# First attention phase of a transformer block: projections and score maxima of a sequence placed within one round, and per-head copies of q and k from SBUF to SBUF

## The reference

```python
x = x + _L0_attn_a_ref(_layernorm(x, axis=-1), L0_attn_a_w_qkv, L0_attn_a_b_qkv, L0_attn_a_w_out, L0_attn_a_b_out)
...
qkv = x @ w_qkv + b_qkv
...
scores = jnp.einsum('bhqd,bhkd->bhqk', q, k) * HEAD_DIM ** (-0.5)
scores = jnp.where(mask[None, None], -jnp.inf, scores)
w = jax.nn.softmax(scores, axis=-1)
return jnp.einsum('bhqk,bhkd->bhqd', w, v)
...
return ctx @ w_out + b_out
```

## Time and profile before

| | before |
|---|---|
| median of 3 runs (lowest to highest) | 3182.99 us (3164.28 to 3186.27) |
| the profiled execution | 3179.51 us, of which the span of the profile is 3177.8 us |
| mean granted clock of PE over the span | 0.923 |
| first attention phase | from 0 to about 1078 us |

### The profile page before, as it was taken

One profiled execution on the slowest core, in us unless ns is written; L12 is line 12 of the kernel. 1 busy time (PEld: TensorE's weight loads), 2 busy tenths in 40 slices (PEclk: granted clock), 3 DMA queues, 4 the chain that ended last, 5 costly groups with the idle time before them and its releaser, 6 DMA issues. The chain is left out here.

```text
span 3177.8 us, 57495 instructions
## 1 busy us (share of the span) xinstructions
PE 2720.7 (86%) x17344; PEld 2117.0 (67%) x17344; DVE 1954.4 (62%) x4975; ACT 1375.7 (43%) x2778; POOL 1426.8 (45%) x1603
## 2 busy tenths in 40 slices
PE   5787787877878678988997999999999949999993
PEld 3554454544555457877996777878787739888872
DVE  6565454654556386766565576777777654566664
ACT  1333233332333224645775434333333317666651
POOL 2332232322233253545732543557575535655556
PEclk9998898988989788989998999999999979999996
DMA  6865666665576445657985222334333248888884
GB/s 202 199 167 145 144 155 154 164 149 141 149 171 161 127 146 206 234 178 245 340 293 176 87 77 65 99 112 126 113 123 110 95 156 295 284 300 307 297 279 150
DMA packets 275022, 565.63 MB, mean 178 GB/s; under 512 B 37152, under 2 KB 144800, under 8 KB 273696
## 3 DMA queue, kind: packets, MB, share of 16 engines
q1 hardware_dynamic: 225568, 427.55, 45.0%
q0 software_dynamic: 49152, 134.28, 12.9%
HBM read 275.96 MB, written 285.21 MB: 177 GB/s over the span
## 5 line engine op out<-in xcount | busy, mean ns | idle before, releaser
L513 ACT ACTIVATE a_pt<-a_S 128x384 f32<-128x384 f32 (+3 forms) x640 | 255.2, 452 | 539.2 <-PE a_S L766 539.0
L428 POOL TENSOR_SCALAR_AFFINE_SELECT a_pt<-a_pt 128x512 f32<-128x512 f32 (+1 forms) x320 | 174.6, 546 | 615.3 <-ACT a_pt L513 615.3
L641 DVE TENSOR_REDUCE a_mx<-a_FB 128x2 f32<-128x384 f32 (+4 forms) x512 | 277.6, 592 | 194.3 <-PE a_FB L744 145.6
L1046 POOL DMA_INDIRECT slots<-f_xn,k_picks x256 | 261.6, 1022 | 249.2 <-PE f_Z L1554 98.1
L1829 POOL DMA_INDIRECT k_yg<-made,k_picks x224 | 223.7, 999 | 255.7 <-PE b_Y L2342 139.1
L2624 POOL DMA_INDIRECT f_yg<-made,k_picks x256 | 257.6, 1006 | 169.9 <-PE f_Z L2817 98.4
L779 PE MATMUL a_PV<-a_pt,a_vv 128*32 128x192 f32 (+4 forms) x2048 | 212.8, 394 | 87.1 <-POOL a_pt L435 87.0
L741 PE MATMUL a_FB<-a_kb,a_qb 128*128 128x192 bf16 (+4 forms) x1024 | 216.3, 277 | 34.5 <-issue 17.4
L766 PE MATMUL a_S<-a_qs,a_ks 97*128 97x384 f32 (+3 forms) x640 | 194.1, 387 | 44.8 <-issue 34.0
L1843 POOL DMA_INDIRECT slots<-b_staged,k_picks x160 | 163.5, 1022 | 103.0 <-issue 39.2
L741 PEld LDWEIGHTS a_FB<-a_kb,a_qb 128*128 128x128 bf16 x1024 | 104.8, 103 | 130.7 <-issue 73.5
(11 more groups left out here) (395 smaller groups left out, 6997.8 us busy)
## 6 DMA issues: line engine op xcount, KB each, us to landing
f_xg<-slots SPq DMA_DIRECT2D x164, 512.0 KB, 6.0
made<-f_ye SPq DMA_DIRECT2D x164, 512.0 KB, 4.0
slots<-a_zeros SPq DMA_DIRECT2D x16, 2560.0 KB, 9.4
a_ks<-a_k_parts SPq DMA_DIRECT2D x96, 256.0 KB, 7.3
a_qs<-a_q_parts SPq DMA_DIRECT2D x192, 128.0 KB, 7.8
a_xin<-in_x SPq DMA_DIRECT2D x16, 512.0 KB, 10.2
a_k_parts<-a_kh SPq DMA_DIRECT2D x32, 256.0 KB, 3.0
a_k_parts<-a_kl SPq DMA_DIRECT2D x32, 256.0 KB, 3.3
```

The costliest lines, as they stand in the source:

```text
L428: ins = nc.gpsimd.affine_select(out=v[:, :, 0:P], in_=v[:, :, 0:P], compare_op=ALU.is_ge, fill=0.0, base=0, pattern=[[0, nh], [1, P]], cha ...
L513: nc.scalar.activation(pt[:, u % 4, b * w:(b + 1) * w], S[:, s_bank[2 * u + b], 0:w], ACT.Exp, scale=DH ** -0.5).then_inc(e_done, 1)
L641: nc.vector.tensor_reduce(mx[:, heads[0]:heads[0] + nh, qb], src[:, 0:nh * n].rearrange("p (h c) -> p h c", c=n), AX.X, ALU.max).then_inc( ...
L1046: nc.gpsimd.indirect_dma_start(out=slots[GROUP1[s]][:, :], out_offset=bass.IndirectOffsetOnAxis(ap=picks[:, i:i + 1], axis=0), in_=xn[:, s ...
```

## The change

Five things are moved or replaced.

1. `timed`: the front of s + 1 now fills slots 0 to 19 of round s (T in 0, q and k in 1 and 2, v in 3 and 4, global maxima from 6, local from 11, mT in 12 and 19), and none of it reaches into round s + 1. The uses stay; global and local maxima alternate less than before.
2. Statistics and normalisation run a round ahead of the front: of sequence s + 2 in slots 12 to 15 of round s. The load of x for s + 2 is still issued in round s.
3. The bf16 copies of q and k go from SBUF to SBUF, one DMA of 16 partitions for each head and each of q and k: 32 DMAs of 16 KB a round (`move_half`) in place of 8 of 128 KB.
4. SP's order in a round is `move_half`, `load_parts(s, 1)`, `store_parts`, `load(s + 2)`, the store of `xres`, `load_parts(s + 1, 0)`, `m_rows(s + 1, 0)`, `clear`, `m_rows(s + 1, 1)`. The wait behind the store of `xres` is now one for the store of the round before.
5. `residual` moves from slot 9 to slot 16. A round -2 is added, which holds only the first normalisation.

```diff
@@ -163,9 +163,9 @@
-    timed = ([(4, ("T", 0)), (4, ("T", 1)), (5, ("q", 0)), (5, ("k", 0)), (6, ("q", 1)), (6, ("k", 1)),
-              (8, ("v", 0)), (9, ("v", 1))] +
-             spread(10, 6.0, MAXG) + [(16, ("mT", 0))] + spread(14, 10.0, MAXL) + [(24, ("mT", 1))])
+    timed = ([(0, ("T", 0)), (0, ("T", 1)), (1, ("q", 0)), (1, ("k", 0)), (2, ("q", 1)), (2, ("k", 1)),
+              (3, ("v", 0)), (4, ("v", 1))] +
+             spread(6, 6.0, MAXG) + [(12, ("mT", 0))] + spread(11, 8.5, MAXL) + [(19, ("mT", 1))])
     timed.sort(key=lambda x: x[0])
     FRONT = [use for _, use in timed]
     NF = len(FRONT)
@@ -173,8 +173,8 @@
-    slot_front = {u: [i for i in range(NF) if timed[i][0] == u] for u in range(2 * NU)}
-    assert timed[-1][0] - NU <= timed[0][0]
+    slot_front = {u: [i for i in range(NF) if timed[i][0] == u] for u in range(NU)}
+    assert timed[-1][0] < NU
     HIGH = [("T", 0), ("T", 1)] + [(c, t) for t in range(QT) for c in ("q", "k")]
@@ -272,11 +271,10 @@
-        STAT_SLOT, VAR_SLOT, LOG_SLOT, GUESS_SLOT, ROOT_SLOT, NORM_SLOT = 0, 0, 1, 2, 3, 3
-        PE_FIRST = (3, 4)
-        RES_SLOT = 9
-        WEIGHTS_SLOT = 4
-        HALF_AT = (5, 6)
+        STAT_SLOT, VAR_SLOT, LOG_SLOT, GUESS_SLOT, ROOT_SLOT, NORM_SLOT = 12, 12, 13, 14, 15, 15
+        RES_SLOT = 16
+        WEIGHTS_SLOT = 17
+        HALF_AT = (1, 2)
         NREADY = 11
@@ -289,15 +287,16 @@
-                body(-1, 1, False, False, True)
-                body(0, 0, False, True, True)
+                body(-2, 0, False, False, False, True)
+                body(-1, 1, False, False, True, True)
+                body(0, 0, False, True, True, True)
                 with eng.Fori(1, nseq - 3, 2) as r:
-                    body(r, 1, True, True, True)
-                    body(r + 1, 0, True, True, True)
-                body(nseq - 3, 1, True, True, True)
-                body(nseq - 2, 0, True, True, True)
-                body(nseq - 1, 1, True, True, False)
-                body(nseq, 0, True, False, False)
+                    body(r, 1, True, True, True, True)
+                    body(r + 1, 0, True, True, True, True)
+                body(nseq - 3, 1, True, True, True, True)
+                body(nseq - 2, 0, True, True, True, False)
+                body(nseq - 1, 1, True, True, False, False)
+                body(nseq, 0, True, False, False, False)
             @block.sync
@@ -320,23 +319,16 @@
-                def store_half(s, t):
+                def move_half(s, t):
                     sp.wait_ge(halved, 2 * QT * s + 2 * (t + 1))
-                    if s >= 2:
-                        sp.wait_ge(half_loaded[t], 32 * (s - 1))
-                    for c, src in (("q", q16), ("k", k16)):
-                        sp.dma_start(half_d[c][s % 2, t * P:(t + 1) * P], src[:, t]).then_inc(half_stored[t], 16)
-
-                def load_half(s, t):
-                    sp.wait_ge(half_stored[t], 32 * (s + 1))
                     if s:
                         sp.wait_ge(f_done, ev(s - 1, NF, m_of[t]))
                     else:
                         sp.wait_ge(w_ready, NREADY)
-                    for c, dst in (("q", qb16), ("k", kb16)):
-                        sp.dma_start(dst[0:DH, HT * t:HT * (t + 1), :],
-                                     half_d[c][s % 2, t * P:(t + 1) * P].rearrange("(h d) n -> d h n", d=DH)
-                                     ).then_inc(half_loaded[t], 16)
+                    for h in range(HT * t, HT * (t + 1)):
+                        r = DH * (h % HT)
+                        for dst, src in ((qb16, q16), (kb16, k16)):
+                            sp.dma_start(dst[0:DH, h, :], src[r:r + DH, t, :]).then_inc(half_loaded[t], 16)
@@ -378,28 +370,26 @@
-                        summed, stored = in_register(sp, ev(s - 1, NTAIL, NTAIL - 1)), in_register(sp, 16 * s)
+                        summed, stored = in_register(sp, ev(s - 1, NTAIL, NTAIL - 1)), in_register(sp, 16 * (s - 1))
+                    if front:
+                        move_half(s + 1, 0)
+                        move_half(s + 1, 1)
                     if core:
                         load_parts(s, 1)
-                    if not isinstance(s, int) or 2 <= s + 2 < nseq:
+                    if front:
+                        store_parts(s + 1, 0)
+                        store_parts(s + 1, 1)
+                    if 2 <= s + 2 < nseq:
                         load(s + 2, par)
-                    if core:
-                        m_rows(s, 1)
-                    if front:
-                        store_half(s + 1, 0)
-                        store_parts(s + 1, 0)
-                        store_half(s + 1, 1)
-                        load_half(s + 1, 0)
-                        store_parts(s + 1, 1)
-                        load_half(s + 1, 1)
                     if tail:
                         at_least(sp, t_dve, summed)
+                        at_least(sp, x_stored, stored)
                         sp.dma_start(rows, xres[:, 1 - par]).then_inc(x_stored, 16)
-                        at_least(sp, x_stored, stored)
                     if front:
                         load_parts(s + 1, 0)
                         m_rows(s + 1, 0)
                         clear(s + 1)
+                        m_rows(s + 1, 1)
@@ -669,26 +653,24 @@
-                def body(s, par, tail, core, front):
+                def body(s, par, tail, core, front, ahead):
                     for u in range(NU):
-                        if front and u == STAT_SLOT:
-                            statistics(s + 1, 1 - par)
-                        if front and u == VAR_SLOT:
-                            variance(s + 1)
-                        if front and u == ROOT_SLOT:
-                            inverse_deviation(s + 1)
-                        if front and u == NORM_SLOT:
-                            normalise(s + 1, 1 - par)
+                        if ahead and u == STAT_SLOT:
+                            statistics(s + 2, par)
+                        if ahead and u == VAR_SLOT:
+                            variance(s + 2)
+                        if ahead and u == ROOT_SLOT:
+                            inverse_deviation(s + 2)
+                        if ahead and u == NORM_SLOT:
+                            normalise(s + 2, par)
                         for i in TAIL_AT.get(u, ()) if core else ():
```

More of the change, by code:

```diff
@@ L233, in phase_a @@
         hilo_d = {c: nc.dram_tensor("a_%s_parts" % c, (2, 2, H, SEQ), F32, kind="Internal").ap() for c in "qk"}
-        half_d = {c: nc.dram_tensor("a_%s_half" % c, (2, H, SEQ), BF16, kind="Internal").ap() for c in "qk"}
         S = ctx.enter_context(nc.psum_tensor("a_S", [P, 3, 512], F32))
@@ L255, in phase_a @@
         halved = sem("halved")
-        half_stored, half_loaded = ([sem("%s%d" % (n, t)) for t in range(QT)] for n in ("half_stored", "half_loaded"))
+        half_loaded = [sem("half_loaded%d" % t) for t in range(QT)]
         parts_stored, parts_loaded = ([sem("%s%d" % (n, t)) for t in range(QT)] for n in ("parts_stored", "parts_loaded"))
@@ L528, in tail_use, with body @@
                     nc.scalar.copy(ch[:, k, :], TL[:]).then_inc(ch_done, 1)
-                def body(s, par, tail, core, front):
+                def body(s, par, tail, core, front, ahead):
                     for u in range(NU):
[L532 to L537, removed]
                         if tail and u == 1:
                             pv_copy(s - 1, 3)
[L541 to L545, removed]
+                        if ahead and u == LOG_SLOT:
+                            log_variance(s + 2)
+                        if ahead and u == GUESS_SLOT:
+                            rsqrt_guess(s + 2)
+                        if isinstance(s, int) and s == -2 and u == WEIGHTS_SLOT:
                             act.wait_ge(w_loaded, W_DMAS)
@@ L558, in body @@
                             tail_use(s - 1, i)
-                        fronts()
+                        for i in slot_front[u] if front else ():
+                            front_use(s + 1, 1 - par, i)
                 nc.scalar.preload_act_table_set("natural_log_exp_and_others")
@@ L606, in halve @@
                 def halve(s, t):
-                    at_least(dve, half_stored[t], ev(s - 1, 32, 31))
+                    at_least(dve, half_loaded[t], ev(s - 1, 16 * 2 * HT, 16 * 2 * HT - 1))
                     for c, dst, src in (("q", q16, qh), ("k", k16, kh)):
@@ L685, in body @@
                             tail_use(s - 1, 1 - par, i)
-                        if isinstance(s, int) and s == -1 and u == WEIGHTS_SLOT:
+                        if isinstance(s, int) and s == -2 and u == WEIGHTS_SLOT:
                             dve.wait_ge(w_high, 2)
@@ L689, in body @@
                             nc.vector.tensor_tensor(wol[:], oraw[:], woh[:].bitcast(F32), ALU.subtract).then_inc(dve_ready, 1)
-                        for i in slot_front[NU + u] if core else ():
```

(7 more changed lines are left out.)

## The result

| | before | changed |
|---|---|---|
| median of 4 runs (lowest to highest) | 3173.64 us (3161.82 to 3186.27) | 3270.35 us (3266.85 to 3273.63) |
| ratio, 95% interval | | 1.0304 (1.0253 to 1.0355) |
| span of the profile | 3177.8 us | 3271.9 us |
| mean granted clock of PE over the span | 0.923 | 0.911 |

The change makes the kernel 3% slower, 97 us, outside the range that was forecast (3085 to 3240).

What follows compares the result with a forecast made beforehand. The load of x, late behind SP's list, was taken as the new bound. Rounds 1 to 13 -10, issue waits -12, start +11, round 14 -8, end -5 sum to -24 us: 3155 us, range 3085 to 3240.

Steps and rivals of the forecast that it cites:

- second rival: A head copy costs 0.63 us like the existing SBUF to SBUF copy: 3230 us; chance 0.22 with its milder form.
- step 2: SP issues 32 head copies at 0.46 us each: 14.7 us of a round, between 10.9 and 20.2.
- the start: Before the loop: 9.5 us more ahead of the first scores, 1.5 in round 0, together +11 us.
- round 14: Loads no x and normalises nothing ahead; loses the POOL wait and two more microseconds: -8 us.
- the end: Round 15 loses the eight late maxima uses and mT: -5 us.
- Step 1: From a round's first score matmul to the first bf16 copy of q and k: 8.75 us.
- Step 3: Nine part loads for slot 12 on SP: 4.1 us, their short wait hidden while x's wait is longer.
- Step 4: Eight stores of parts on SP at 0.46 us each: 3.7 us, then the load of x is issued.
- Step 5: The load of x lands 10.0 us after its issue, with DVE's statistics in slot 12 waiting for it.
- Step 6: Statistics and the negation `a_mTg` on DVE once x has landed: 3.0 us.
- Step 7: The rest of the round on DVE, 15.3 us, then the last mT, 0.5 us.
- POOL's wait: The residual waits for the store of `xres`, delaying PE's mask; moved to slot 16, 6.05 us a round go.

Runs made afterwards that it cites:

- x first: The changed kernel with the load of x at the head of SyncE's list, ahead of the 32 copies: 3192.52 us, ratio 1.0054.
- both first: The changed kernel with the part loads and then the load of x ahead of the 32 copies: 3053.1 us, ratio 0.962.
- parts first: The changed kernel with the nine part loads for slot 12 at the head of SyncE's list: 3157.97 us, ratio 0.9937.

## Why the prediction was wrong

The path was the right one: the seven steps from a round's first score to the next stand in the trace in their order. The forecast fell by one price, which was named as the second rival's, and by smaller sizes beside it. The sum had -24 us where the spans differ by +94. Of these 118 us, 84 are step 2 in 13 rounds, 18.5 the start, 9.4 round 14 and 1.3 the end (forecast -5, measured -3.7); the remaining 4 are the other steps of the rounds less what the loop's turns gave back.

- Step 1, to the first head copy 8.75 us: 9.3.
- Step 2, 32 head copies at 0.46 us, 14.7: **this step failed.** They are issued at 0.63, and the step lasts 21.2 us with a stutter. I chose the row nearest in shape, the part loads out of DRAM; the row nearest in source, the SBUF to SBUF copy of `a_mTg` with 0.63, had the price. The experiment with 32 loads from DRAM shows that the route decides, both ends in SBUF. Over 13 rounds 6.5 us each make 84 us, and the second rival had 75 for it.
- Step 3, part loads 4.1 us: 4.9. That their lateness hides in the wait for x was half right. PE stands still for both, 10.0 and then 3.9 us in round 12, and behind the second one it has more to catch up. The orders of the list show that each of the two alone would hold the round. If the wait for x goes, the parts were to cost up to 3 us a round; with x first they cost 9.7 (65.0 us against 55.3 with both first), of which the price of step 2 can account for 6.5.
- Step 4, eight stores 3.7 us: 4.1. Step 5, landing of x 10.0 us: 8.9. Step 6, 3.0 us: 3.1. Step 7, the rest 15.8 us: 16.7.
- Sum for a round away from the loop's turns: 60.4 forecast, 68.2 measured (round 12), of which 6.5 are step 2.
- POOL's wait went as forecast. Its worth did not: 6.05 us a round were counted, and 9.0 were to be had (116.6 us in 13 rounds of the experiment with the residual alone). In the changed kernel that gain was never paid out, since the new stalls lower the clock as the old one did: 0.86 in rounds 1 to 13 against 0.89 before.
- The issue waits at the loop's turns were forecast to lose 12 of 51.4 us. Instead of 34.0 and 17.4 us the trace shows 16.8 us in 5 waits, put down to `a_mTl`. The direction was right, the gain larger. The five stand at the heads of rounds 3, 5, 7, 9 and 11, where the turns are. In the kernel with both first two of the same five are put down to issue again (10.4 us), so they are most likely still the turn, though the profile does not settle it.
- The start was forecast at +11 us and came to +29.5: 15.0 ahead of round 0, where the 32 copies at 0.63 us take 5.4 more than the price used, and 14.5 in round 0, where I had allowed 1.5. Its waits are 4.0 us for the copies, 7.9 at the scores of slot 12 and 5.5 for the negation, and I had counted only the copies for it.
- Round 14 was forecast at -8, as it loads no x. It came to +1.4. PE stands 10.0 us there at the scores of slot 12, and with no wait for x beside it the whole length shows.

The rule of the Trainium skill that was weighed (DMA: Bandwidth & Descriptors, Rules for kernel authors: join many small transfers) came true. The trace puts the overhead at 0.63 us of SyncE's time for a copy; the transfers themselves landed 1.8 us after their issue at the median. Joining two in one took 153 us off, but only 16 once the two needed loads stood ahead of the copies (3053.1 against 3036.7). The section of the Trainium skill on the anatomy of one DMA, on the same page, from which the prediction worked out an estimate of 3.2 us for x, describes DMAs issued by GpSimd; x is issued by SyncE here and the lowest median of its landing in any run was 4.1 us.

## What to carry to other kernels

An issuing engine's list is a path like any other: count the issues ahead of each transfer that someone waits for, price them by a row with the same source and destination, and put what is needed first at its head. Here moving two entries ahead of 32 small copies was worth 217 us, with the copies still there. A short stall of the matrix engine cost more than its length here, since the granted clock fell behind it (78.7 us of stalls, 116.6 us of time); and before a large rework, its smallest part may be worth trying alone, as one slot number gave 4% here, and the intervals of the best reworked kernels overlap with it.

## What was not expected of the hardware

- Issuing a DMA from SBUF to SBUF took 0.63 us of SyncE's time, whether it moved 16 or 32 KB; a DMA of the same 16 KB from DRAM took 0.46. The issue of a store of 128 KB from SBUF to DRAM lasted 0.34 to 0.43.
- Taking 78.7 us of stalls from PE in 13 rounds also took 37.5 us from the busy time of the same matmuls, as the granted clock went from 0.89 to 0.95; in the kernels with both loads first it was 0.98.
- The landing time of the same load of 512 KB went from 4.1 to 12.5 us with what stood ahead of it on SyncE's queue: 4.1 at the head of the list (x first), 4.9 behind 32 copies and eight stores (parts first), 8.3 right behind nine part loads (both first), 8.4 behind copies, nine loads and eight stores (changed), 12.5 the same with the bf16 copies through DRAM. Why the last is the longest was not tried. In this order, with size and median to landing:

```profile
a_xin<-in_x SPq DMA_DIRECT2D x16, 512.0 KB, 4.1
a_xin<-in_x SPq DMA_DIRECT2D x16, 512.0 KB, 4.9
a_xin<-in_x SPq DMA_DIRECT2D x16, 512.0 KB, 8.3
a_xin<-in_x SPq DMA_DIRECT2D x16, 512.0 KB, 8.4
a_xin<-in_x SPq DMA_DIRECT2D x16, 512.0 KB, 12.5
```
